# A last stage with its loop written out and half a batch's output product moved behind attention's

## The reference

```
x = norm(x + linear_attention_and_mlp(x))
x = norm(x + moe_64_experts_top8(x))                       # capacity 64, and a shared expert
x = norm(x + grouped_attention(x))                         # groups of 32 tokens
x = norm(x + moe_8_experts_top2(x))
```

```
z = layernorm(x);  v, gate = split(silu(z @ Wh + bh));  qk = silu(z @ Wqk + bqk)
quad_q, lin_q, quad_k, lin_k = four scaled and shifted copies of qk
attn = square(relu(quad_q @ quad_k.T / G + bias)), causal inside a group
out  = gate * (attn @ v + lin_q @ cumsum over earlier groups of (lin_k.T @ v / G))
x3   = norm(x + (out @ Wout + bout + x))
scores = softmax(x3 @ Wg.T);  the best two of eight, made to sum to 1 -> comb
for e in range(8):
    a, b = split(x3 @ W1[e].T + b1[e]);  acc += comb[:, e] * a * sigmoid(b)
y = norm(x3 + acc @ Wo.T + bo * sum(comb))
```

## Time and profile before

| | |
|---|---|
| median of 3 runs | 661.34 us (659.84, 661.34, 911.91) |
| profiled execution | 657.42 us, its span 655.7 us |
| PE busy, granted clock | 569.0 us (87%), mean 0.893 |
| DVE busy | 462.2 us (70%) |
| POOL busy | 433.6 us (66%) |
| ACT busy | 307.1 us (47%) |
| chain that ended last | PE 44%, DVE 21%, issue 8%, POOL 6%, ACT 2% |

### The profile page before, as it was taken

How to read it: one execution, slowest core, us unless ns; L and a number is a source line. 1 busy time by engine, 2 the same in 40 slices (tenths; PEclk the granted TensorE clock), 3 DMA queues, 4 the chain that set the end, 5 groups by cost and what they waited for, 6 DMA issues and landing times.

```text
span 655.7 us, 10938 instructions
## 1 busy us (share of the span) xinstructions
PE 569.0 (87%) x3157; PEld 457.7 (70%) x3157; DVE 462.2 (70%) x1557; ACT 307.1 (47%) x825; POOL 433.6 (66%) x478
## 2 busy tenths in 40 slices
PE   5988888799257977998999999998999999999993
PEld 4777777655146755776787887876878778788762
DVE  1558788879959322495768878776788787886873
ACT  2547766549202111223454736645556465563450
POOL 6453454318575666537787979977979799752673
PEclk9979999889655555589999999998999999999997
DMA  4697756659420112062130030300302100000000
GB/s 129 161 279 281 284 203 235 271 143 239 85 73 29 53 53 60 32 237 96 53 129 1 19 127 9 137 2 9 136 0 72 72 9 8 1 17 0 9 9 17
DMA packets 47225, 62.01 MB, mean 95 GB/s; under 512 B 13026, under 2 KB 39873, under 8 KB 46146
## 3 DMA queue, kind: packets, MB, share of 16 engines
q1 hardware_dynamic: 44610, 56.15, 27.0%
q0 software_dynamic: 2560, 5.23, 2.7%
HBM read 35.16 MB, written 24.13 MB: 90 GB/s over the span
## 4 chain that ended last, share of the span: by engine, by line
PE 44%; DVE 21%; issue 8%; POOL 6%; ACT 2%; DVEq 0%; DMA 0%; POOLq 0%; ACTq 0%
PE pair L1413 7%; PE pair L1415 7%; PE pair L1414 7%; PE pair L1738 5%; POOL c_acc L935 3%; DVE cand L1934 3%; PE pair L1748 2%; DVE c_g L1214 2%; DVE keyT L1936 2%; PE pair L2044 2%; PE pair L1527 2%; PE pair L1522 2%; PE pair L1461 1%; PE pair L1452 1%; DVE slot_key L1945 1%
## 5 line engine op out<-in xcount | busy, mean ns | idle before, releaser
L935 POOL TENSOR_TENSOR c_acc<-c_acc,c_g 128x512 f32<-128x512 f32 x112 | 144.5, 1291 | 22.9 <-DVE c_g L1214 16.1
L1071 ACT ACTIVATE c_sg<-pair 128x256 f32<-128x256 f32 x256 | 94.9, 384 | 78.9 <-PE pair L1415 75.8
L1214 DVE SCALAR_TENSOR_TENSOR c_g<-pair,c_comb,c_sg 128x256 f32<-128x256 f32 x224 | 99.5, 476 | 22.5 <-ACT c_sg L1071 18.3
L1413 PE MATMUL pair<-c_w_hi,c_x3h 128*128 128x512 f32 x256 | 109.2, 427 | 4.2 <-DVE c_acc L1214 3.1
L1415 PE MATMUL pair<-c_w_hi,c_x3l 128*128 128x512 f32 x256 | 100.9, 394 | 0.0
L1414 PE MATMUL pair<-c_w_lo,c_x3h 128*128 128x512 f32 x256 | 100.7, 394 | 0.0
L1413 PEld LDWEIGHTS pair<-c_w_hi,c_x3h 128*128 128x128 f32 x256 | 48.2, 188 | 18.8 <-DVE c_g L1214 7.5
L1415 PEld LDWEIGHTS pair<-c_w_hi,c_x3l 128*128 128x128 f32 x256 | 48.1, 188 | 11.4
L1414 PEld LDWEIGHTS pair<-c_w_lo,c_x3h 128*128 128x128 f32 x256 | 48.3, 189 | 7.5
L1816 POOL DMA_INDIRECT routed_rows<-x1T_all,dest_row x32 | 31.8, 993 | 26.6 <-DVE x1T_all L1728 19.0
L1811 POOL DMA_INDIRECT rows_all<-token_rows,tok_row x32 | 31.3, 977 | 14.8 <-issue 9.4
(11 more groups left out here) (374 smaller groups left out, 1507.6 us busy)
## 6 DMA issues: line engine op xcount, KB each, us to landing
routed_rows<-rows_all SPq DMA_DIRECT2D x8, 2048.0 KB
c_c<-routed_rows SPq DMA_DIRECT2D x7, 2048.0 KB, 7.8
token_rows<-a_xw SPq DMA_DIRECT2D x8, 384.0 KB, 2.8
a_x<-in_L_attn_x SPq DMA_DIRECT2D x8, 256.0 KB, 3.4
base_all<-a_xw SPq DMA_DIRECT2D x8, 256.0 KB, 3.7
c_c<-routed_rows SPq DMA_DIRECT2D x4, 512.0 KB, 4.8
out<-c_outb SPq DMA_DIRECT2D x16, 128.0 KB, 1.8
wgu_late<-in_L_ffn_w_gate SPq DMA_DIRECT2D x4, 480.0 KB, 7.2
```

The source lines that it names most:

```text
L935: g.tensor_tensor(acc, acc, b["g"][:, (2 * uf + i) % 4, :, :], ALU.add).then_inc(s["acc"], 1)
L1071: a_.activation(b[f"sg{q % 2}"][:, x, :], self.pair[q % 2][:, x, H1:2 * H1], SIG).then_inc(s["sig"], 1)
L1214: v.scalar_tensor_tensor(out=dst, in0=self.pair[q % 2][:, x, 0:H1], scalar=b[f"comb{uf}"][:, j * E1 + e:j * E1 + e + 1], in1=b[f"sg{q % 2} ...
L1413: t.matmul(dst, w_hi, x_hi, start=start, stop=False)
```

## The change

Four edits. The loop of stage C becomes a Python loop, so that its four bodies are written out with constant counts. On PE, `half_output(f, uf, 0)` moves behind attention's output product in slot 9. On DVE, `half_sum(f, uf, 0)` moves from slot 9 to slot 10, where it stands behind x3's norm. In `first_pass` the statistics of y move behind both gated products. `landing` gets 128 cells, since written-out code uses more of them.

```diff
-AT = dict(zT=0, accT=(8, 1), out=(9, 2), gate=2, y4=(9, 3), quads=3, ...
+AT = dict(zT=0, accT=(8, 1), out=(9, 2), gate=2, y4=(10, 3), quads=3, ...
...
         body(eng, 0, 1, r=2, a=1, f=0)
-        with eng.Fori(0, (B - 4) // 2) as i:
-            k = 2 * i
+        for k in range(0, B - 4, 2):
             body(eng, 1, 0, r=k + 3, a=k + 2, f=k + 1, t=k)
             body(eng, 0, 1, r=k + 4, a=k + 3, f=k + 2, t=k + 1)
...
             v.tensor_tensor(b["goT"][:, 0, :], Y[:, :], b["gateT"][:, 0, :], ALU.mult).then_inc(s["go"], 1)
-            dve.wait_ge(s["y"], r + 1)
-            v.memset(self.landing(), 0.0)
-            stats("r", b["y"], r + 1)
             prod(0, 4, bank[1], b["gateT"][:, 1, :])
             dve.wait_ge(s["prod5"], 5)
             dve.wait_ge(s["av_mm"], 2)
             v.tensor_tensor(b["goT"][:, 1, :], Z[:, :], b["gateT"][:, 1, :], ALU.mult).then_inc(s["go"], 1)
+            dve.wait_ge(s["y"], r + 1)
+            v.memset(self.landing(), 0.0)
+            stats("r", b["y"], r + 1)
...
                 if t_ is not None and q == place("out", 1, a):
                     half_output(t_, ua, 1)
-                if f is not None and q == place("out", 0, a):
-                    half_output(f, uf, 0)
                 if a is not None:
                     if q == AT["v"]:
...
                         ins.then_inc(s["w_mm"], 1)
+                if f is not None and q == place("out", 0, a):
+                    half_output(f, uf, 0)
+                if a is not None:
                     if q == AT["x3T"]:
...
-        landing_all = sb("landing", [P, 96])
-        cells = iter(range(96))
+        landing_all = sb("landing", [P, 128])
+        cells = iter(range(128))
```

More of the change, by code:

```diff
@@ L49 @@
 NROWS = 5 + 4 + 4 + E1 + 4 * E1
-AT = dict(zT=0, accT=(8, 1), out=(9, 2), gate=2, y4=(9, 3), quads=3, gate2=3, v=4, outb=(15, 5), sim=6, off=7, atd=6, av=8, w=9, x3=10, x3T=12, lg=13, y=7, z=11)
+AT = dict(zT=0, accT=(8, 1), out=(9, 2), gate=2, y4=(10, 3), quads=3, gate2=3, v=4, outb=(15, 5), sim=6, off=7, atd=6, av=8, w=9, x3=10, x3T=12, lg=13, y=7, z=11)
 ALONE = dict(accT=10, out=11, y4=12)
```

## The result

On one chip the changed kernel took 666.77 us (median of 9 runs, 662.66 to 674.57) against 661.31 us for the kernel before (median of 9): ratio 1.0075, 95% interval 1.0047 to 1.0103. It is slower, by 5.5 us or 0.8%, where 660.5 was forecast. The time lies inside the range of 655 to 667, near its upper end. Run again later on a third chip, where the kernel before takes 641.91 us, the ratio was 1.0104 (1.0057 to 1.0151).

What follows compares the result with a forecast made beforehand. PE, busy 87% of the span, was taken to bound the kernel, with DVE behind it. Terms -4.6 - 1.1 + 6.8 = +1.1 us gave 658.5 or 661.7 by base; forecast 660.5 us, range 655 to 667.

Steps and rivals of the forecast that it cites:

- the sum: Whole kernel: loop -4.6, first pass -1.1 and the two moves +6.8 us make +1.1 us, with no clock falls.
- rival 2: PE's new 1.6 us wait before slot 13's `up` lets the clock fall, 1.60 us per such body; chance 0.20.
- The chance: Clock fall in PE's new wait before slot 13: put at 0.20, deciding where idle time nears 2 us.
- The price: Cost of one clock fall, from product stretches behind the loop's branch and at its exit: 1.60 us a body.
- the lighter part of rival 2: Clock falls at slot 13 in one to three bodies: 660 to 663 us, up to 666 on the other base.
- The moves' steady price: Slots 9 and 10: DVE waits 0.97 us for attention's output, x3l comes later; +6.8 us over seven bodies.
- Rival 1: DVE's order costs nothing and PE's wait for x3 goes: 0.76 us gained a body, 646.4 to 650; chance 0.07.
- The loop: Stage C's loop written out: branch stall and register work go, -4.6 us, between -3.9 and -5.3.
- The first pass: y's statistics behind both gated products: PE's second output product starts sooner, x3's inverse root too; -1.1 us.
- Rival 3: Loop's stall stays or returns as code waits in four bodies: +5.0 us, 662.4 or 665.6; chance 0.10.
- The base: Time before: 657.42 us profiled, or 660.6 mean of two timings; 660.5 taken near the middle of 658.5 and 661.7.

Runs made afterwards that it cites:

- the filled kernel: Changed kernel plus seven unused 512-wide PE products behind x3's transposes, against the kernel before: 642.52 us, ratio 0.9978; on the third chip 641.94 us, ratio 0.9988.

## Why the prediction was wrong

**The step that failed** is the sum's missing term for the clock, and with it rival 2 as it was set off against the forecast: that PE's new wait of 1.6 us would leave the clock alone, with 0.20 for a fall, at 1.60 us each. The place, the wait and the mechanism were named and came as written (the wait measured 1.74 us); chance and price were wrong, and both on the same side. The runs showed falls in three of seven bodies, at 2.75 us each.

- *The chance.* It was read from two rows: a fall after 2.20 us, none after 1.95, "decides near 2 us". One event on each side is no threshold, and the other runs overturn it: behind the same wait of 1.95 us in the first pass the clock fell in the loop alone and in the moves alone. Behind 1.73 and 1.74 us at slot 13 it fell in 3 of 7 bodies, twice; in the moves alone it fell in 4 of 7 (1.79 to 1.92 us), and not behind 1.80 at a branch. What the clock does after such a wait varies from body to body with the same rows around it. The mean number of falls is what a forecast needs, and ten falls in these 21 bodies say that with seven such waits a run the case without any is the unlikely one.
- *The price.* 1.60 us was the difference of two stretches behind the branch. There the clock was low for 3.4 us, which the trace before shows (PE's busy time, granted clock behind it):

```profile
450.00:452.00 2.00, 2.00 (x7) 0.63 0.00 0
452.00:454.00 2.00, 2.00 (x8) 0.51 0.00 0
```

Behind slot 13's `up` it was low for 6.8 us in each of the ten falls, in a stream of products at 0.43 instead of 0.23 us each, and 2.75 us were lost. Per us at the low level the two prices are near each other, 1.60 / 3.4 = 0.47 and 2.75 / 6.8 = 0.40: what the forecast had too small is the length of the low stretch. Where DVE's move alone made it 3.4 us again, a fall cost 1.1. Why it is 3.4 us in one place and 6.8 in another stays open.
- Three falls of 2.75 on top of the prediction's sum of +1.1 would be +9.3 us, and the medians differ by 5.5. The other terms were off by some 2 us the other way, next. How many bodies fell in the runs that have no profile is not known, so the remainder isn't shared out. That the time still lies inside the range is owed to the room left there for the lighter part of rival 2, and in part to luck, since the two errors go against each other.

**The moves' steady price** was right: 0.97 us a body forecast, 42.3 - 41.4 = 0.9 in the periods, 7.5 us in the medians of the filled kernel and the one without moves (6.8 forecast). Rival 1, that the order costs nothing, is refuted by the same runs.

**The loop** was -4.6 forecast and is -6.3 us in the medians (ratio 0.990, an interval of 4.4 to 8.8 us, which holds the forecast). In the profiles it is as forecast: first to last output product is 253.06 us before and 594.41 - 345.82 = 248.59 in the loop-and-first-pass version, -4.5 over six periods. **The first pass** was -1.3 in the timeline for -1.1. Both together gave -8.8 us on the first chip and -7.5 on the third for the -5.7 forecast; the filled kernel, which should be at +1.1, came out at -1.9 and at 0.0. A part of these 2 us is the first pass's own fall: behind the wait of 1.95 us that the change takes away, the clock fell in two of the three profiles that have it, at some 1.2 us each, and the term of -1.1 counted only the wait. Where the rest lies is not settled: one profile of before can't show how often its own clock falls.

**Rival 3** (the stall stays or comes back) is refuted by the loop alone. The rule quoted of the Trainium skill ("Runtime: NRT & Kernel Launch", Instruction fetch mechanics), that straight code is prefetched, agrees with every version here that has no loop: DVE shows no gap at the former branch in any of them.

**The base** moved the forecast by little, but it turned its sign: the median of before was 661.31 again, so the sum of +1.1 by it was 662.4. The 660.5 that was forecast says faster than before where the sum says slower, which was careless; the kernel is slower.

## What to carry to other kernels

Price a move by what the engine behind does in its new wait, and then by what follows that wait on TensorE: a new idle time of 1.7 us in a stream of full products cost 0.9 us steadily and 2.75 more whenever the clock fell, which three of seven times it did. Take the price of a fall from its low stretch, and don't take one wait after which the clock held for proof that it will hold again. If such a wait can't be avoided, fill it with products that nobody reads (it saved 9 us here); better, leave the order alone where the engine ahead (DVE here) has no room, since the wait only moves. And take the parts of a change one by one: two of three parts here together made the kernel 1.3 to 1.5% faster, and the third ate all of it.

## What the runs showed of the hardware

- The granted clock fell in some bodies and not in others behind the same wait of 1.74 us between the same instructions. By kernel, falls in seven bodies by PE's waits in slots 12 and 13: 0.75 us alone, none (six profiles without the moves, the loop's branch apart); 1.73 to 1.74, three and three; the moves with the loop, four, all behind 1.79 to 1.92, and none in its three with 1.74; 1.15 us, none; 0.76 and 1.74 with transposes between, six; 1.66 and then 0.75 with full products between, none; filled, none (twice). At the branch back it fell after 2.20 and 1.91 us and not after 1.80; in the first pass after 1.95 us in two profiles and not in a third. The shortest wait ahead of a fall was 1.46 us, in the first pass after.
- The low stretch lasted 6.8 us behind slot 13 in the changed kernel and in the moves alone, ten times, and 3.4 us at the branch, behind the first pass's 1.95 us, and in the six bodies with DVE's move alone. Ahead of the first pass's attention it was 6.8 us in the changed kernel and 3.4 in the version without the moves. What sets bodies of one kernel apart stays open, as does what sets these lengths. The Trainium skill ("TensorE: Matmul & The Clock Gate", Part 1) describes the clock gate as watching an activity window that runs freely and isn't reset by the kernel, so that the moment of a change varies between runs. Bodies that differ with the same rows around them fit that; no run here shows the window itself.
- A branch back at the end of a long body left DVE idle for 2.76 us, and for 2.46 in the moves alone and in the first pass alone, with no releaser; written out, that idle time is gone.
- The three chips differ by 2.7% in the time of the same kernel before (659.31 against 641.91 us), and most of it lies ahead of these bodies: the first attention output product of the same kernel without the moves starts at 345.82 us on the one and at 331.45 on the other.
